# Splitting experts in other turns and slots, and gating two images at a time, in a conv, attention and mixture-of-experts kernel

## What is computed

```python
x = x + conv(group_norm(x))          # 1x1 conv over channels and 28 local correlations
t = tokens(x)                        # 8 x 256 tokens of 192
t = t + attention(layer_norm(t))     # causal, one head, 8 sequences of 256
t = t + experts(layer_norm(t))       # 8 experts, top 1
# experts, for a token f:
gate = f @ Wg.T + bg                 # 8 logits, idx = argmax
out  = (silu(f @ W1[idx].T) * (f @ W2[idx].T)) @ W3[idx].T     # inner width 469
```

## Time and profile before

| | |
|---|---|
| median of 3 runs | 261.23 us (259.09 to 263.37) |
| the profiled execution, own time | 260.33 us |
| its span, first to last instruction | 258.4 us |
| TensorE matmul, busy | 205.8 us, 80% |
| VectorE, busy | 173.0 us, 67% |
| ScalarE, busy | 116.0 us, 45% |
| GpSimd, busy | 105.0 us, 41% |
| mean granted TensorE clock | 0.905 of 2.4 GHz |

### The profile page before, as it was taken

How to read it: one execution, slowest core, us unless ns; L and a number is a source line. 1 busy time by engine, 2 the same in 40 slices (tenths; PEclk the granted TensorE clock), 3 DMA queues, 4 the chain that set the end, 5 groups by cost and what they waited for, 6 DMA issues and landing times.

```text
span 258.4 us, 4928 instructions
## 1 busy us (share of the span) xinstructions
PE 205.8 (80%) x1338; PEld 183.1 (71%) x1338; DVE 173.0 (67%) x564; ACT 116.0 (45%) x235; POOL 105.0 (41%) x124
## 2 busy tenths in 40 slices
PE   0595879999769889889772306999999999999970
PEld 0494778888567777778562305799999999999960
DVE  2676769563566796787888442677778778768651
ACT  1457455333657875785650201334343343343320
POOL 3144423520384389688888630031231331313331
PEclk9999599999979999999855555999999999999996
DMA  6981632348005236347530112233221000000000
GB/s 204 385 262 40 195 106 63 111 117 372 6 0 211 48 165 241 58 183 241 129 131 16 63 37 67 71 81 89 60 62 33 16 19 9 30 18 18 28 14 0
DMA packets 15733, 25.84 MB, mean 100 GB/s; under 512 B 3767, under 2 KB 12659, under 8 KB 14688
## 3 DMA queue, kind: packets, MB, share of 16 engines
q1 hardware_dynamic: 13840, 22.40, 27.3%
q0 software_dynamic: 1872, 3.18, 3.6%
HBM read 19.50 MB, written 6.76 MB: 102 GB/s over the span
## 4 chain that ended last, share of the span: by engine, by line
PE 53%; DVE 17%; DMA 9%; issue 8%; ACT 6%; POOL 4%; DVEq 1%; POOLq 1%; SPq 0%; ACTq 0%
PE bank L1244 7%; PE bank L988 4%; PE bank L1220 4%; PE bank L990 4%; PE bank L989 4%; PE bank L992 4%; PE bank L991 4%; PE bank L1245 3%; DMA stage<-in_w_all 3%; PE bank L1235 2%; DMA near_rows<-gram 2%; PE bank L983 2%; DMA taps_sb<-near_rows 2%; PE bank L1097 2%; PE bank L1139 1%
## 5 line engine op out<-in xcount | busy, mean ns | idle before, releaser
L450 POOL DMA_INDIRECT out_rows<-yo,rows x23 | 22.4, 974 | 81.2 <-DVE yo L955 56.3
L1244 PE MATMUL bank<-wall,HH 128*128 x92 | 29.4, 375 | 1.5 <-DVE HL L935 1.5
L940 DVE TENSOR_TENSOR gh<-gh,bank 128x470 f32<-128x470 f32 x23 | 14.8, 645 | 21.5 <-PE bank L992 21.5
L614 ACT ACTIVATE HH<-bank 128x512 fp32r<-128x512 f32 x23 | 13.8, 599 | 27.6 <-PE bank L1220 27.6
L1245 PE MATMUL bank<-wall,HL 128*128 x92 | 23.1, 251 | 0.0
L405 POOL DMA_INDIRECT token_rows<-rows,posi x16 | 19.0, 1188 | 8.7 <-issue 6.5
L620 ACT ACTIVATE FH<-bank 128x256 fp32r<-128x256 f32 x23 | 8.9, 385 | 29.1 <-PE bank L1235 27.7
L423 POOL TENSOR_TENSOR wall<-stage,wall 128x940 fp32r<-128x940 f32 x8 | 17.5, 2191 | 10.2 <-DVE posi L828 5.9
L988 PE MATMUL bank<-wall,FH 128*128 x46 | 19.8, 430 | 1.0 <-DVE FL L943 1.0
L617 ACT ACTIVATE gh<-bank 128x470 f32<-128x470 f32 x23 | 13.0, 565 | 13.4 <-PE bank L992 13.4
L1244 PEld LDWEIGHTS bank<-wall,HH 128*128 128x128 f32 x92 | 17.3, 188 | 1.8 <-issue 1.7
(11 more groups left out here) (212 smaller groups left out, 663.4 us busy)
## 6 DMA issues: line engine op xcount, KB each, us to landing
stage<-in_w_all SPq DMA_DIRECT2D x8, 1324.0 KB, 6.7
rows<-token_rows SPq DMA_DIRECT2D x23, 98.0 KB
near_rows<-gram SPq DMA_DIRECT2D x8, 243.0 KB, 3.0
xcm<-in_x_cm SPq DMA_DIRECT2D x2, 768.0 KB, 8.3
rows<-in_x_tm SPq DMA_DIRECT2D x1, 1536.0 KB, 14.0
token_rows<-emptyt SPq DMA_DIRECT2D x1, 882.0 KB, 5.1
taps_sb<-near_rows SPq DMA_DIRECT2D x8, 103.0 KB, 2.1
small_sb<-in_small SPq DMA_DIRECT2D x1, 704.0 KB, 8.1
```

The lines of the kernel that those rows point to most:

```text
L450: pool.indirect_dma_start(out=out, out_offset=bass.IndirectOffsetOnAxis(ap=rows[:, j, C + 2:C + 3].bitcast(U32), axis=0), in_=yo[:, par], ...
L1244: nc.tensor.matmul(dst[:, 0:2 * C], HH[:, 1 - par, k], w(0, P, c0, c0 + 2 * C), start=(k == 0), stop=False)
```

## The change

- Gate and positions run on VectorE in turns 4, 6, 8, 9 and 10, for the images (0, 1), (2, 3), (4, 5), 6 and 7 (`GATED`). TensorE still makes each image's gate logits in turn t = image + 3, into columns of its own; the counting matmuls of a pair are 14 in place of 5.
- GpSimd scatters a pair's tokens together, after the root of that turn: four indirect transfers in turns 4, 6 and 8, two in 9 and 10.
- Experts are split in turns 1, 2, 6, 7, 8 (experts 0 to 4), expert 5 after turn 10 (on GpSimd and VectorE after the table), experts 6 and 7 in slot steps 0 to 4 (`SPLIT_AT`, `GAP_EXPERT`, `SPLIT_SLOT`). Turns 3, 4 and 5 split none on ScalarE and GpSimd. A leftover comes one turn after its expert's high parts.
- SP loads expert 7's weights after the rows of the fourth slot.
- TensorE waits, at the head of slot step j, until j + 1 experts are split, and not before the first slot until all are. So that slot j can only need the experts 0 to j, an expert without tokens gets one slot (the maximum with 1 in the table).
- The loops over turns and slots are written out on all engines.

```diff
+GATED = {4: (0, 1), 6: (2, 3), 8: (4, 5), 9: (6,), 10: (7,)}
+PAIR = 2 * HALVES
+SPLIT_AT = {1: 0, 2: 1, 6: 2, 7: 3, 8: 4}
+GAP_EXPERT = 5
+SPLIT_SLOT = {0: 6, 2: 7}
...
+            def weights_again(e):
+
                 sp.wait_ge(wall_lo, e - 1)
                 sp.wait_ge(wall_q, e - 1)
                 weights_in(e)
+
+            for e in range(2, 7):
+                weights_again(e)
...
+            for j in range(SLOTS):
+                load_slot(j, j % 2, j // 2 if j > 1 else None)
+                if j == 3:
+                    weights_again(7)
...
-                if t >= 3:
-                    pool.wait_ge(pos_ready, t - 2 + AHEAD)
-                if t <= EXPERTS:
-                    weights_lo(t - 1, 1 - t % 2)
+                gated = GATED.get(t, ())
+                if gated:
+                    pool.wait_ge(pos_ready, gated[-1] + 1 + AHEAD)
+                if t in SPLIT_AT:
+                    for part in range(2):
+                        weights_lo(part, SPLIT_AT[t])
                 if t <= IMAGES:
                     token_root(t - 1)
-                if t >= 3:
-                    scatter_tokens(t - 3)
+                for b in gated:
+                    scatter_tokens(b)
             pool.sem_inc(yo_free, AHEAD)
+            pool.wait_ge(table_ready, 1)
+            for part in range(2):
+                weights_lo(part, GAP_EXPERT)
...
             for j in range(SLOTS):
                 send_slot(j, j % 2)
+                for part in range(2):
+                    if j - 1 - part in SPLIT_SLOT:
+                        weights_lo(part, SPLIT_SLOT[j - 1 - part])
...
+            for t in range(1, IMAGES + 3):
+                step(t, t % 2)
+            for part in range(3):
+                weights_hi(part, GAP_EXPERT)
...
+            for j in range(-1, SLOTS + 1):
+                ffn_step(j, j % 2, j > 0, 0 <= j < SLOTS, j < SLOTS - 1)
+                for part in range(3):
+                    if j - part in SPLIT_SLOT:
+                        weights_hi(part, SPLIT_SLOT[j - part])
...
+            def leftover(e):
+
+                ve.wait_ge(wall_hi, e + 1)
+                w = wall[CB:P, e, 2 * W12:3 * W12]
+                nc.vector.tensor_tensor(w, stage[CB:P, e % 2, W12:2 * W12], w.bitcast(F32), ALU.subtract).then_inc(wall_q, 1)
...
+                gated = GATED.get(t, ())
+                n = HALVES * len(gated)
+                wide = [P, n, EXPERTS]
+
+                def logits(v):
+                    return v.rearrange("p (h e) -> p h e", e=EXPERTS)
+
+                def each(v):
+                    return v.rearrange("p (h a) -> p h a", a=1).to_broadcast(wide)
+
+                if gated:
+
+                    ve.wait_ge(g_ready, gated[-1] + 1 + AHEAD)
+                    g, m = lg[:, 0:n], gmx[:, 0:n]
+                    link(nc.vector.tensor_tensor(g, logits(bank[7][:, 0:n * EXPERTS]), logits(c2("bg")[:, 0:n * EXPERTS]), ALU.add))
+                    link(nc.vector.tensor_reduce(m, g, AX_X, ALU.max))
+                    link(nc.vector.tensor_tensor(g, g, each(m), ALU.is_ge))
+                    link(nc.vector.tensor_tensor(g, g, logits(c2("desc")[:, 0:n * EXPERTS]), ALU.mult))
+                    link(nc.vector.tensor_reduce(m, g, AX_X, ALU.max))
+                    nc.vector.tensor_tensor(oh[:, 0:n], g, each(m), ALU.is_equal).then_inc(oh_ready, len(gated))
...
+                if t - 1 in SPLIT_AT:
+                    leftover(SPLIT_AT[t - 1])
+                if gated:
+
+                    ve.wait_ge(pf_ready, gated[-1] + 1 + AHEAD)
                     r1 = run[:].rearrange("p (h e) -> p h e", h=1).to_broadcast(wide)
-                    link(nc.vector.tensor_tensor(lg[:], bank[7][:, 2 * EXPERTS:4 * EXPERTS].rearrange("p (h e) -> p h e", h=2), r1, ALU.add))
-                    link(nc.vector.tensor_tensor(lg[:], lg[:], oh[:], ALU.mult))
-                    nc.vector.tensor_tensor(run[:], run[:], bank[7][:, 4 * EXPERTS:5 * EXPERTS], ALU.add)
-                    link(nc.vector.tensor_reduce(pos[:], lg[:], AX_X, ALU.add))
+                    at = PAIR * EXPERTS
+                    link(nc.vector.tensor_tensor(g, logits(bank[7][:, at:at + n * EXPERTS]), r1, ALU.add))
+                    link(nc.vector.tensor_tensor(g, g, oh[:, 0:n], ALU.mult))
+                    nc.vector.tensor_tensor(run[:], run[:], bank[7][:, 2 * at:2 * at + EXPERTS], ALU.add)
+                    link(nc.vector.tensor_reduce(pos[:, 0:n], g, AX_X, ALU.add))
                     hold()
-                    nc.vector.tensor_copy(posi[:, bass.ds(2 * t - 6, 2)], pos[:]).then_inc(pos_ready, 1)
+                    nc.vector.tensor_copy(posi[:, HALVES * gated[0]:HALVES * gated[0] + n], pos[:, 0:n]).then_inc(pos_ready, len(gated))
...
-            nc.vector.tensor_copy(tiles_f[:], tiles_i[:])
-            link(nc.vector.tensor_copy(ends[:, 0], tiles_i[:]))
+            nc.vector.tensor_scalar(tiles_f[:], tiles_i[:], 1.0, None, ALU.max)
+            link(nc.vector.tensor_scalar(ends[:, 0], tiles_i[:], 1.0, None, ALU.max))
...
             nc.vector.memset(gh[:, :, FE:FT * P], 0.0)
+            leftover(GAP_EXPERT)
...
+            for j in range(-1, SLOTS + 1):
+                ffn_step(j, j % 2, j > 0, 0 <= j < SLOTS, j < SLOTS - 1, j // 2 + 2 if j + 2 < SLOTS else None)
+                if j - 2 in SPLIT_SLOT:
+                    leftover(SPLIT_SLOT[j - 2])
...
+                    first = next(p[0] for p in GATED.values() if t - 3 in p)
                     pe.wait_ge(x2_copied, t - 2 + AHEAD)
-                    pe.wait_ge(pos_ready, t - 3 + AHEAD)
+                    pe.wait_ge(pos_ready, first + AHEAD)
                     wg = c2("wg")
                     for h in range(HALVES):
-                        dst = bank[7][:, EXPERTS * h:EXPERTS * (h + 1)]
+                        c0 = EXPERTS * (HALVES * (t - 3 - first) + h)
+                        dst = bank[7][:, c0:c0 + EXPERTS]
                         nc.tensor.matmul(dst, x2T[:, 0, P * h:P * (h + 1)], wg[:, 0:EXPERTS], start=True, stop=False)
                         mm = nc.tensor.matmul(dst, x2T[:, 1, P * h:P * (h + 1)], wg[:, EXPERTS:2 * EXPERTS], start=False, stop=True)
...
-                    e += EXPERTS
-                    nc.tensor.matmul(bank[7][:, e:e + EXPERTS], all_, oh[:, 0], start=True, stop=False)
-                    nc.tensor.matmul(bank[7][:, e:e + EXPERTS], all_, oh[:, 1], start=False, stop=True).then_inc(pf_ready, 1)
+                    for h in range(n + 1):
+                        e = EXPERTS * (PAIR + h) if h < n else EXPERTS * 2 * PAIR
+                        for k in range(h):
+                            mm = nc.tensor.matmul(bank[7][:, e:e + EXPERTS], all_, oh[:, k], start=(k == 0), stop=(k == n - 1))
+                        if h < n:
+                            mm = nc.tensor.matmul(bank[7][:, e:e + EXPERTS], before, oh[:, h], start=(h == 0), stop=True)
+                    mm.then_inc(pf_ready, len(gated))
...
+                    pe.wait_ge(wall_lo, min(j + 1, EXPERTS))
+                    pe.wait_ge(wall_q, min(j + 1, EXPERTS))
```

More of the change, by code:

```diff
@@ L306, in _ @@
             weights_in(1)
-            for e in range(2, EXPERTS):
+            def weights_again(e):
                 sp.wait_ge(wall_lo, e - 1)
@@ L492, in copy_taps, with weights_hi @@
                 nc.scalar.activation(tapsT[:, b % 2], bank[5][0:TAPS, 0:PIX], ACT.Copy).then_inc(taps_copied, 1)
[L494 removed]
+            def weights_hi(part, e):
+                par = e % 2
                 if part == 0:
[L497 removed]
+                    if e > 0:
                         sc.wait_ge(conv_taken, IMAGES)
[L499 to L501 removed]
+                    sc.wait_ge(stage_in[par], 16 * (e // 2 + 1))
+                w = wall[:, e]
                 if part == 0:
@@ L523, in take_v, with step @@
                 nc.scalar.activation(V[:, par].rearrange("p h c -> p (h c)"), bank[2][:, 0:HALVES * C], ACT.Copy).then_inc(v_copied, 1)
-            def step(t, par, loaded):
-                if isinstance(t, int) and t == 2:
+            def step(t, par):
+                e = SPLIT_AT.get(t)
+                if t == 2:
                     sc.wait_ge(ln1_ready, 3)
@@ L598, in _ @@
             sc.wait_ge(empty_out, 16)
-            for t in range(1, 3):
-                step(t, t % 2, (t - 1) // 2 + 1)
-            with sc.Fori(1, IMAGES // 2 - 1) as i:
-                for u in range(2):
-                    step(2 * i + (u + 1), 1 - u, i + 1)
-            for t in range(IMAGES - 1, IMAGES + 3):
-                step(t, t % 2, (t - 1) // 2 + 1 if t <= EXPERTS else None)
+            for t in range(1, IMAGES + 3):
+                step(t, t % 2)
+            for part in range(3):
+                weights_hi(part, GAP_EXPERT)
             sc.preload_act_table(ACT.Silu)
@@ L875, in _ @@
             ve.sem_inc(dve2, LINKS)
-            step(1, 1, False)
+            step(1, 1)
             take_conv(IMAGES - 1)
@@ L880, in _ @@
```

(15 more changed lines are left out.)

105 lines of the change are left out of this document (28 added, 77 removed).

## The result

The changed kernel takes 267.9 us (median of 4 runs, 266.98 to 268.84), the kernel before 260.48 beside it (4 runs, 259.09 to 263.37): 1.030 times as long, 95% interval 1.022 to 1.038, so slower. The profiled execution took 266.98 with a span of 265.2, against 260.33 and 258.4.

A forecast was written before the change was run, and what follows sets the result against it. It took a ring of waits through VectorE and TensorE to bound the middle turns, GpSimd's program order the stage's end, and TensorE's stream the slots. 260.33 + 1.9 (middle) + 1.9 (slots) = 264.1; forecast 264.3, range 257.5 to 268.5 us.

The forecast's parts named there:

- the range's end: Whole kernel: 268.5 us, from the forecast with slots at 3.7, +1 for the code and 0.9 to the median.
- Three signs: Among the signs of a wrong forecast: slot-row normalisation over 0.38, middle turns of 8 us, slot stage over 102.3 us.
- Early turns, -1.8: Turns 3 to 6: pairing and loop heads gain 0.4, 0.2, 1.05 and 0.3, less 0.15; bounds 0.8 and 5.4.
- first rival: Turns 3 to 6 shorten to TensorE's own work, -5.4 instead of -1.8 at turn 6; total 260.5; chance 0.17.
- its objection: Early turns: in every second turn the next subtraction stands behind the positions, which wait for TensorE.
- the fourth: Rival: early turns give nothing but loop heads; 265.3, or 267.3 with a late expert 7 load; chance 0.16.
- Turns 7 to 10, +1.9: GpSimd's program order, 16.6 us of work after image 3's positions, makes the last transfer end 1.9 later.
- second rival: GpSimd doesn't hold turn 8; 257.9, or 254.3 with early turns at TensorE's work; chance 0.09 alone, 0.06 both.
- Handover, 0: Landing to first slot's rows keeps its length; splitting expert 5 fits VectorE's idle 3.63; otherwise up to 0.8.
- Slots, +1.9: Slot steps: leftovers 0.4 each and a 1.1 stall for expert 7 before step 7; bounds 0.8 and 3.7.
- third rival: GpSimd's subtractions block VectorE's normalisation of slot rows, 0.9 an expert, 1.8 in all; total 266.1; chance 0.10.
- Written-out code, 0: Writing out the loops costs 0 beyond the loop heads counted in the early turns; bounds 0 and +1.

The follow-up runs named there:

- e7: The changed kernel with expert 2 split in turn 3 and expert 3 in turn 6, none in turn 7; 262.82 us, 1.008 times the kernel before.
- e1: The changed kernel with images gated singly and one expert split in each of turns 1 to 8, as the kernel before; 261.65 us, ratio 1.006 to that kernel.
- e3: The changed kernel with images gated one at a time as before, keeping the late splits; 264.83 us, 1.018 times the kernel before.
- e9: e8_best with the first half of expert 5's GpSimd subtraction moved ahead of the wait for turn 8's positions; 258.62 us, 0.989 times the kernel before.
- e2: The changed kernel with pairs kept but one expert split in each of turns 1 to 8, none later; 266.42 us, 1.019 times the kernel before.
- e8_best: The changed kernel with experts 0 to 5 split in turns 1, 2, 3, 4, 6, 8, expert 6 after the table, expert 7 before first-slot products; 259.70 us, ratio 0.996.

## Why the prediction was right in the middle stage and short in the slots

267.9 us lies near the upper end of the range, 257.5 to 268.5; slower by over 2% had been given 0.30, and within 2%, with 264.3, was the likelier. That it lies inside is luck in part. The slots cost 5.3, more than their upper bound of 3.7, and the terms named for the range's end (260.33 + 1.9 + 3.7 + 1 + 0.9) give 267.8 and not 268.5. Three signs that the prediction had named for its being wrong are there: a normalisation longer than 0.38, a slot stage over 102.3 and middle turns of under 8 us.

**Early turns, -1.8: the sum was right, its parts were not.** -1.87 measured, against the bounds 0.8 and 5.4. Turns 3 to 6 take 7.76, 9.68, 7.56 and 9.87 us, and took 9.07, 9.63, 9.05 and 9.22 before. The free turns 3 and 5 gain 1.3 and 1.5, where I had 0.4 and 1.05; the paired turns 4 and 6 lose 0.05 and 0.65, where I had gains of 0.2 and 0.3. That the two errors cancel is luck. In free turn 5 TensorE is busy for all but 0.11 us, as the first rival had it for all four turns:

```profile
98.29:105.85 7.56, 7.45 (x59) 6.32 (x59) 4.34 (x17) 4.50 (x11) 3.09 (x5) 1.00 0.05 17
```

In the paired turns, as its objection said, the next turn waits for the positions. So the first rival holds for the free turns alone, and the fourth (loop heads alone) is out.

**Turns 7 to 10, +1.9: right.** The last transfer ends at +1.7, taken from turn 2, and the stretch with no gap stands as I worked it out: 115.64 to the root's end at 132.27, 16.6 us. One thing came in another place: I had turn 8's gate chain finished by then, but its one-hot was held for 4.39. It cost nothing, since the rows behind it waited another 0.97 for the root. The second rival is out. e7 shows what the wait was worth: with expert 2 split in turn 3 the middle falls by 3.7.

**Handover, 0: small miss.** From the end of the last transfer to the first product 7.18 us against 6.78, 0.4 more. 0.3 of it is the first normalisation, 0.67 long: it started at 156.79 and ended 0.11 after GpSimd's second part of expert 5 (155.55 + 1.80). GpSimd came to that part late because its first one had waited in its turn for VectorE's leftover (152.43, 1.14):

```profile
152.47 3.11 POOL L431 TENSOR_TENSOR wall<-stage,wall 128x940 fp32r<-128x940 f32 x1
```

**Slots, +1.9: this step failed; +5.3 measured.** The terms, with heads of steps from TensorE's timeline:

- Step 3, with ScalarE's two parts and the first leftover: 0.49 against 0.4.
- Steps 5 and 6: 1.95 + 1.80 = 3.75, where I had 0.4 (second leftover) and 1.1 (expert 7). Of step 6's 1.80 the wait for expert 7 is 1.56; it was forecast at 1.1 (by that sum's own terms 187.8 + 0.4 - 186.44 - 0.8, 0.96). Step 5's 1.95 is what the forecast lacked. The third rival had this mechanism: VectorE's normalisation held by GpSimd's subtractions. It was priced at 0.9 an expert from 1.4 of the first hold and 0.2 of the second. The holds are 1.3 and 1.6. The first costs next to nothing where the rival had 0.7 (step 4 takes 3.98), and the leftover lies behind the second, so that their sum less VectorE's slack of 0.76 is left over: 1.55 + 1.14 - 0.76 = 1.93.
- Step 0: 0.52, not forecast: the granted clock stays at its lower level for nearly the whole first step (0.56 against 0.65 in the windows above). The step takes 4.59 in e1 as before, 4.88 in e3, 4.75 in e9 and 5.10 or 5.11 in all others. In e2, which splits nothing after turn 8, it is 5.10, so it takes no split behind the table to get it; no run isolates what sets it. Step 1 +0.15, the remaining steps +0.15 and what follows the last step's head +0.28.

The sum is 0.49 + 3.75 + 0.67 (steps 0 and 1) + 0.4 (the rest) = 5.3.

The error was one of reading. I gave the third rival 0.10 because of the earlier trace rows: a normalisation at 131.48 beside a GpSimd copy at 131.51, both at their usual length. That copy moves 4 columns in 0.19 us and says little of a subtraction of 940 columns that reads two rows for 2.2 us. It could not even have shown a hold: the copy ends at 131.70, a held normalisation would end some 0.13 later, 131.83, and one that isn't held ends at 131.48 + 0.38 = 131.86. The same group of rows held the better witness, a comparison stretched from 0.17 to 2.66. The Trainium skill (SBUF - State Buffer, Who interferes with whom) says that a VectorE instruction in two-port mode contends with GpSimd, and one with two SBUF inputs with a GpSimd instruction that reads SBUF, and that the loser blocks until the other ends. The trace agrees: 1.71 to 2.01 for the normalisation, to 0.13 of the subtraction's end. I ranked one row of a trace above this rule although the row was of another size of instruction.

**Written-out code, 0 (bounds 0 and +1).** e1 is 0.6% longer, some 1.6 us, with an interval from 0.4 to 2.9; 0.7 of it is in the middle and 0.1 in the slots of its profile, the rest is not located. 1.6 lies above the bound of +1, and the interval reaches below it. The Trainium skill (Runtime: NRT & Kernel Launch, Instruction fetch mechanics) calls written-out code the cheaper; the trace agrees where the loops stood, turns 3 to 6 with 36.23 us against 36.97, about the 0.8 of loop heads that I had counted. What e1 loses comes behind them, with the longer first transfers.

The total: 264.1 from the sum, 266.98 in the profiled execution, 267.9 by the median. The 2.9 between the first two are 3.4 of the slots and 0.4 of the handover, less 0.2 of the middle, 0.65 by which turn 2 started earlier and 0.15 outside the span.

## What to carry to other kernels

Work moved off one engine's busy stretch has to be placed against the idle time of the same engine, and together with what else the change adds there. With pairs, the middle was 91.9 us with a split in each turn, 87.9 with turns 3 to 5 free and a gapless 16.6 us behind them, and 84.2 with one expert moved back into the free turns; with single images it was 86.5, 86.4 and, well placed, 84.5. Before giving GpSimd work beside VectorE, list the VectorE instructions that will run under it: here the element-wise ones that read only SBUF waited until GpSimd's subtraction was done, and what matters is the slack of the instruction behind them. And when a rule speaks against a change, a row may only outweigh it if it shows the same kinds and sizes.

## What the runs showed of the hardware that was not expected

- A hold can last over two GpSimd instructions: the one-hot that reads two SBUF tiles took 4.39 us, from 126.95 to 131.34, over L431 and L434, which end at 131.28. It had started 0.39 before L431, while an indirect transfer was issued (126.35, 0.98). It need not last over both: in e8_best GpSimd's first part started 0.02 before VectorE's larger leftover, the leftover came in after it, and GpSimd's second part then waited for the leftover:

```profile
150.57 2.16 POOL L429 TENSOR_TENSOR wall<-stage,wall 128x940 fp32r<-128x940 f32 x1 [0.17 <-issue]
152.69 2.69 POOL L432 TENSOR_TENSOR wall<-stage,wall 128x768 fp32r<-128x768 f32 x1
```

```profile
150.59 3.13 DVE L764 TENSOR_TENSOR wall<-stage,wall 64x940 fp32r<-64x940 f32 x1
```

- BATCH_NORM_STATS2, which reads one SBUF tile, is not held: 0.62 for two at 136.14 in e9_half_first while L432 runs (135.17 to 136.98), the rows above.
- GpSimd's side is held too, and the order of starting decides. The first indirect transfer of a batch takes 1.93 to 2.10 us wherever VectorE's leftover (two SBUF inputs, 1.14) started 0.10 to 0.30 before it (139.04 and 139.18 in e9_half_first: 1.97). It takes 1.08 to 1.10 where the leftover started between 0.02 before and 0.13 after it, and 1.09 to 1.26 without one. In the slots an output transfer takes 1.22 and not 0.97 at the end of a leftover (174.74, the leftover from 173.97).
